# Decoder layer on one core: the load of the second batch's values is made to wait for the new pair's first exponential

## The reference

```python
# B = 32 batches, 56 text rows, 16 query heads on 8 key/value heads, context (1500, 128)
scores = einsum('bhtd,bhsd->bhts', q, k) / sqrt(128)
scores = where(mask, scores, -inf)
attn   = softmax(scores)
out    = einsum('bhts,bhsd->bhtd', attn, v)
x      = layernorm(x + out_heads @ Wo)
```

## Time and profile before

| what | us |
|---|---|
| median of 3 runs | 2003.5 (2000.5 to 2003.97) |
| the profiled execution | 2002.64 |
| its span in the profile | 2000.8 |
| PE busy | 1855.4 (93%) |
| DVE busy | 1276.7 (64%) |
| ACT busy | 934.7 (47%) |
| POOL busy | 623.4 (31%) |
| DMA, mean over the span | 64 GB/s |

### The profile page before, as it was taken

How to read it: one execution, slowest core, us unless ns; L and a number is a source line. 1 busy time by engine, 2 the same in 40 slices (tenths; PEclk the granted TensorE clock), 3 DMA queues, 4 the chain that set the end, 5 groups by cost and what they waited for, 6 DMA issues and landing times. The chain is left out here.

```text
span 2000.8 us, 35238 instructions
## 1 busy us (share of the span) xinstructions
PE 1855.4 (93%) x10628; PEld 1651.2 (83%) x10628; DVE 1276.7 (64%) x3469; ACT 934.7 (47%) x1646; POOL 623.4 (31%) x360
## 2 busy tenths in 40 slices
PE   7899789998999999999989999999999985999998
PEld 6788679898988889898987989898888974888887
DVE  4654567776766777676667767776676755545554
ACT  4333355555545455555545555554555542323221
POOL 1210353333435243334425333343523107210010
PEclk9999889999999999999999999999999996999999
DMA  4233642432324142232324233232413005000000
GB/s 169 83 119 123 155 74 72 78 58 57 58 54 79 53 87 38 77 58 53 64 66 87 37 76 62 54 58 61 89 45 49 14 14 155 21 28 10 9 19 10
DMA packets 99093, 128.68 MB, mean 64 GB/s; under 512 B 36239, under 2 KB 79921, under 8 KB 98833
## 3 DMA queue, kind: packets, MB, share of 16 engines
q1 hardware_dynamic: 60067, 112.74, 24.3%
q10 hardware_dynamic: 38912, 14.80, 3.5%
HBM read 107.22 MB, written 20.30 MB: 64 GB/s over the span
## 5 line engine op out<-in xcount | busy, mean ns | idle before, releaser
L789 ACT CAST b_pT_hi<-b_turn 125x512 fp32r<-125x512 f32 (+1 forms) x768 | 406.6, 531 | 633.7 <-PE b_turn L729 619.2
L883 DVE TENSOR_TENSOR b_pT_lo<-b_turn,b_pT_hi 125x512 fp32r<-125x512 f32 (+1 forms) x768 | 478.5, 624 | 230.3 <-ACT b_pT_hi L789 223.5
L869 DVE CUSTOM_DVE_ANT_0 b_p<-b_score,b_mask_add 128x500 f32<-128x500 f32 x672 | 452.1, 674 | 187.9 <-issue 69.3
L729 PEld LDWEIGHTS b_turn<-b_ident,b_p 128*125 128x125 f32 x2688 | 415.9, 189 | 59.6 <-issue 1.1
L729 PE MATMUL b_turn<-b_ident,b_p 128*125 128x128 f32 x2688 | 423.8, 275 | 0.9 <-ACT b_p L795 0.9
L746 PE MATMUL b_out<-b_pT_hi,b_c_hi 125*128 125x512 f32 (+1 forms) x768 | 352.7, 459 | 73.7 <-DVE b_pT_lo L883 73.5
L795 ACT ACTIVATE b_p<-b_p,b_shift 128x1500 f32<-128x1500 f32 x224 | 347.4, 1551 | 18.8 <-DMA rden_store<-b_rden 9.7
L1010 POOL TENSOR_TENSOR b_oT_lo<-b_oT,b_oT_hi 128x896 fp32r<-128x896 f32 x32 | 67.7, 2115 | 738.2 <-ACT b_oT_hi L817 738.2
L747 PE MATMUL b_out<-b_pT_lo,b_c_hi 125*128 125x512 f32 (+1 forms) x768 | 285.3, 372 | 0.0
L748 PE MATMUL b_out<-b_pT_hi,b_c_lo 125*128 125x512 f32 (+1 forms) x768 | 284.9, 371 | 0.0
L715 PE MATMUL b_score<-b_cT_hi,b_q_hi 128*128 128x500 f32 x672 | 268.1, 399 | 9.5 <-DVE b_cT_lo L956 9.5
(11 more groups left out here) (175 smaller groups left out, 2854.4 us busy)
## 6 DMA issues: line engine op xcount, KB each, us to landing
cT_in<-in_ctxT SPq DMA_DIRECT2D x32, 750.0 KB, 11.7
b_c_in<-in_ctx SPq DMA_DIRECT2D x32, 750.0 KB
q_store<-a_fold_in_or_q_stage SPq DMA_DIRECT2D x16, 896.0 KB, 4.0
q_in<-q_store SPq DMA_DIRECT2D x32, 448.0 KB, 10.0
b_rden_all<-rden_store ACTq DMA_DIRECT2D x32, 256.0 KB, 4.2
b_rden_all<-rden_store ACTq DMA_DIRECT2D x32, 192.0 KB, 3.8
b_mask_in<-in_mask SPq DMA_DIRECT2D x32, 187.5 KB, 10.7
c_w_in<-in_hidden SPq DMA_DIRECT2D x16, 256.0 KB, 3.1
```

What stands on the lines that cost most here:

```text
L729: mm = pe.transpose(turn_bank[n % 3][0:CK, u * 128:(u + 1) * 128], p[slot % 2][:, u, c * CK:(c + 1) * CK], ident[:])
L789: act.copy(pT_hi[:, n % 3, 0:w], turn_bank[n % 3][0:CK, 0:w]).then_inc(hi_done, 1)
L869: dve.tensor_tensor_reduce(out=p[slot % 2][:, u, keys], in0=score_bank[j][:, 0:FW], in1=mask_add[:, b, keys], scale=1.0, scalar=-3.0e38, o ...
L883: dve.tensor_tensor(pT_lo[:, n % 3, 0:w], turn_bank[n % 3][0:CK, 0:w], pT_hi[:, n % 3, 0:w].bitcast(F32), ALU.subtract).then_inc(lo_done, 1)
```

## The change

```diff
@@ phase_b, block.sync @@
             def loads(i, first=False):
                 load_q(i, 0)
                 load_scores(i, 0)
                 load_values(i, 0)
                 load_q(i, 1)
                 load_scores(i, 1)
                 if not first:
                     store(i - 2)
                 residual(i - 1)
+                sp.wait_ge(exp_done, PUNITS * i + 1)
                 load_values(i, 1)
```

## The result

| | median, us | ratio to before |
|---|---|---|
| before (4 runs beside it) | 2003.3 | |
| with the change (4 runs, 2025.0 to 2032.3) | 2029.5 | 1.0131 [1.011, 1.0152] |

The change makes the kernel slower by 1.3%. The forecast was 1955, and 2029.5 lies above its range of up to 2015; rival B, "the store becomes the new bound", is what happened. The profiled execution has a span of 2027.5, where before had 2000.8.

The account below looks back on a forecast made before the run. DVE's instruction fetch, delayed at each loop jump by the values load, was taken to stall PE. Gaining 73 us there and losing 24 at the reciprocals' store gave -49 us from about 2003.5, so 1955, range 1926 to 2015.

Parts of the forecast that it names:

- rival B: At ACT's reciprocals' store: landing 17 us or more after issue makes it the new bound, 2020 to 2053 us; chance 0.16.
- What bounds the kernel: At DVE's loop jump: instructions wait behind the values load, stopping PE 4.53 us and lowering its clock; 86 us in all.
- Step 1: At the 14 loop jumps: with values issued later, DVE waits 3.7 us and PE idles 0.9; 73 us gained.
- Step 2: At the values' new issue time: ACT's reciprocals' store lands in 14 us, costing 1.6 us in 15 pairs; 24 us lost.
- The meetings of pair 0: Two earlier stores issued near large loads in pair 0, which let ACT go on 19 and 16 us later.
- From the hold to PE: At ACT's wait for the store: a 3 us hold of ACT costs PE about 1.0 us.
- The clock: After PE's new stall at the store: the clock falls in some pairs, costing 0.6 us on the average.
- Step 3: At POOL's use of the moved loads: values, queries, keys and mask still arrive in time; cost 0.
- A: At the reciprocals' store: its elements slip ahead of the values on all 16 engines, no cost; 1930 or 1917 us; chance 0.25.
- Rival C: At DVE's jump: the values don't hold the instructions, one row delays them 0.23 us; 2003 to 2027 us; chance 0.12.

Follow-up runs that it names:

- e1: The changed kernel with the values load waiting for the pair's second exponential instead of its first; ratio to the kernel before 0.9715.
- e3: The changed kernel with the next pair's queries, keys and mask also held, until the fifth exponential, so the values alone meet the store; ratio 0.983.
- e9: The changed kernel with ACT's load of the last slot's reciprocals moved two steps later in its program; ratio 0.9814.
- e2: The changed kernel with the values load waiting for DVE's first scores of the pair instead of the first exponential; ratio 0.9725.
- e4: The kernel before, without the new wait, its values load cut into 112 and 13 partitions, carried by 16 and 13 DMA engines; ratio 0.985.
- e5: The changed kernel with its values load cut into 112 and 13 partitions, carried by 16 and 13 DMA engines; ratio 0.9696.
- e6: The kernel before with the same wait instruction added, on a count reached a pair earlier, so it never holds anything; ratio 1.0014.

## Why the prediction was wrong, step by step

**What bounds the kernel: right.** e1 took away the wait at the jump without the long stop at the store, and gained 56 us.

**Step 1, the jump: right to its size.** DVE idles 3.6 us on the average, 3.7 forecast; PE 0.83 us, 0.9 forecast; no fall of the clock. 63.4 - 11.7 = 51.7 us of waiting are gone, and 14 stretches at the lower clock, 51.5 us of work in all of which half is lost, 25.8: **77 us gained**, 73 forecast.

**Step 2, the landing of the store: the failed term, and with it the price of 24 us.** "I take 14 us, between the free one and the 16 us of the meeting with as few elements." It was 18.3. Its parts, one by one:

- "On the 11 engines without values it should be through ... on the 5 others its elements alternate with rows of values": eleven by 9 to 11 us and five late; this was so.
- The price of that: 14 us is what e3 measured, 14.2, with the values alone. The queries, keys and mask behind them, 1.4 of the 2.1 MB that the step itself counts, add 3.0 to 4.1 us and were not in the 14. The step let them come too late to matter, which it had reasoned for the 11 engines alone. On the five others 80 of the 125 packets were still to come when the bulk began to flow (at 1038.15), and in the crowd a row of values then took 0.36 us on the average, where it took 0.24 in e3. For some 16 rows on each engine that is about 2 us of the 3 to 4. The meetings of pair 0 had said 16 and 19; the 14 taken lay under both, and no row stood for it.
- From the hold to PE: "ACT is held 3 us, PE about 1.0 us" is what e9 shows, 2.9 and 0.7. The conversion was right and was fed the wrong hold. Of a hold of 7.1 to 8.2 us PE loses all but the first 3 us or so.
- The clock: 0.6 us on the average was forecast, and it was 31.6 us over 14 stalls, 2.3 each, more than the 1.6 taken from the earlier trace rows, since half of the low stretches last 6.83 us.

Sum of it: 67.6 us in 15 stops (13 in the loop's pairs with 61.2, pair 1 with 4.7, the last with 1.7) and 31.6 of clock, **99 us lost**, 24 forecast. 99 - 77 = 22 us. Pair 0 got 2.5 better. PE's busy time grew by 11.8 us, of which these stops explain 31.6 - 25.8 = 5.8; the other 6 lie outside them, 3.4 of them in one stretch of low clock at 55 us, in a stage that the change doesn't reach; where the rest comes from was not traced. 22 - 2.5 + 6 = 25.5, against 26.7 measured in the span.

**Step 3: right.** POOL's two waits for `b_c_in` are those of the start, 12.9 us.

**The rivals.** B had its mechanism and its place right, and the time lay inside its 2020 to 2053. Its point of decision was set a little low: a hold costs PE all but 3 us of it, so a loss of 4.9 us per pair (3.3 of waiting and 1.6 of clock) is a landing at about 17 us and not 16. 18.3 is over both. Its chance of 0.16 rested on "it had more elements, and the values were a microsecond ahead", as reasons for a kinder landing. The second is no such reason: the last pair of e2 has the values 4.6 us ahead and no load behind them, and its store lands after 8.2 us, while those that come with the values land after 17 to 18. A had slipping ahead right for 11 engines of 16; for the rest it would have needed the store ahead by e1's 5 us, or spread values.

Rival C's price for its rule, 0.23 us, took a packet for one row of values. The rule of the Trainium skill that it cites ("DMA: Bandwidth & Descriptors", "Queues, rings and completion order") is a round robin by packets, too, but counts some 9 to 17 descriptors to a packet. The trace decides for the store: one element and one row take turns. For the instructions one row is too little: the runs show 2.6 us on one chip and 3.8 on the other.

**What stays open.** No run here tells why the large loads all but stop while the parts of a store of small elements are outstanding (its packets have started within 2 us, its parts land 6 to 10 us after the issue). Nor does one tell why the instructions still wait on values that are spread over all engines (e4, 5.6 us), or what makes up the rest of the crowd's 3 to 4 us.

## What to carry to other kernels

Moving a large load away from one victim moves it onto another: before pricing the gain, look in the trace at what will be in flight at the new moment, and price the meeting with every load that is released behind the moved one. A small-element store whose completion stands at the head of an engine's queue is such a victim; give it a lead, spread the large load over all DMA engines, or put its waiter later in the program. Each of the three was worth 3 to 4% against the change as it was made. The first only moved the meeting once more, onto the load of the reciprocals, at a smaller price.

## What the runs showed of the hardware

- A transfer of 125 partitions went over 5 DMA engines, and a store issued with it landed in two groups, 11 parts by 9 to 11 us and 5 at 13 to 19 us. On those 5 engines one 4-byte element of the store and one row of 6144 bytes took turns. Cut into 112 and 13 partitions it left the store alone (10.1 us).
- A store of 384 4-byte elements took 8 to 10 us to land with no large load about. While it was under way, large loads moved at 19 to 49 GB/s in the trace of the change (45 to 89 in e5's), and at 251 GB/s once its first eleven parts had landed.
- DVE's jump to the start of its loop took 3.4 to 3.8 us with no large load about, and 5.2 to 8.2 us with the values under way.
- The same kernel before differs by 1.2% between chips, and the contended jump by 1.3 us (7.5 in before, 6.2 in e6); the ratio of the change was the same on both, 1.013.
